# The W of two value heads in two PSUM banks, each with its own copy and its own count

## What is computed

```python
def step(S, xs):
    qt, kt, vt, gt, bt = xs
    S = S * jnp.exp(gt)[..., None, None]
    kS = jnp.einsum('bhk,bhkv->bhv', kt, S)
    S = S + bt[..., None, None] * kt[..., :, None] * (vt - kS)[..., None, :]
    o = jnp.einsum('bhk,bhkv->bhv', qt, S)
    return (S, o)
...
o = o * jax.lax.rsqrt(var + 1e-06) * norm_w * _silu(z)
return o.reshape(B, T, value_dim) @ W_out
```

## Time and profile before

| what | value |
|---|---|
| median of 3 runs | 2559.62 us (2553.06 to 2559.69) |
| the profiled execution, its own time | 2561.94 us |
| its span, first to last instruction | 2559.9 us |
| TensorE products busy | 2189.3 us (86%) |
| VectorE busy | 1676.1 us (65%) |
| ScalarE busy | 961.1 us (38%) |
| GpSimd busy | 701.5 us (27%) |
| chain that ended last | PE 44%, DVE 12%, ACT 3%, issue 3% |

### The profile page before, as it was taken

One profiled execution on the slowest core, in us unless ns is written; L12 is line 12 of the kernel. 1 busy time (PEld: TensorE's weight loads), 2 busy tenths in 40 slices (PEclk: granted clock), 3 DMA queues, 4 the chain that ended last, 5 costly groups with the idle time before them and its releaser, 6 DMA issues.

```text
span 2559.9 us, 41273 instructions
## 1 busy us (share of the span) xinstructions
PE 2189.3 (86%) x13086; PEld 1568.3 (61%) x13134; DVE 1676.1 (65%) x2777; ACT 961.1 (38%) x2492; POOL 701.5 (27%) x598
## 2 busy tenths in 40 slices
PE   3089989968884687799999999999999999999996
PEld 2044445433334343587787778778778778778776
DVE  7267777740014555678777777777877777777775
ACT  0000000017761001454454454455455445445444
POOL 8000000000001002342552452353354255245243
PEclk8589999989995799899999999999999999999998
DMA  2510000000000011000000000000000000000001
GB/s 63 57 37 18 18 31 23 20 7 0 0 0 20 27 31 54 21 13 29 25 18 23 25 33 12 29 25 12 29 25 12 29 25 12 29 25 24 17 25 33
DMA packets 24766, 61.01 MB, mean 24 GB/s; under 512 B 3315, under 2 KB 9731, under 8 KB 22563
## 3 DMA queue, kind: packets, MB, share of 16 engines
q1 hardware_dynamic: 24742, 60.72, 8.2%
HBM read 56.31 MB, written 4.40 MB: 24 GB/s over the span
## 4 chain that ended last, share of the span: by engine, by line
PE 44%; DVE 12%; ACT 3%; issue 3%; POOL 0%; DMA 0%; DVEq 0%; ACTq 0%; POOLq 0%
PE ps L1103 5%; PE ps L1231 4%; PE ps L1223 4%; PE ps L1141 4%; PE ps L1151 3%; DVE P L1634 3%; DVE P_term L1631 3%; DVE conv L1555 2%; PE ps L1288 2%; PE ps L1166 2%; PE ps L1277 2%; PE ps L1237 2%; PE ps L1177 2%; PE ps L1290 2%; PE ps L1264 2%
## 5 line engine op out<-in xcount | busy, mean ns | idle before, releaser
L1555 DVE SCALAR_TENSOR_TENSOR conv<-raw,tap_st,conv 128x1024 f32<-128x1024 f32 x204 | 300.0, 1470 | 3.8
L517 DVE TENSOR_REDUCE m_part<-ps 128x512 f32 (+3 forms) x384 | 208.3, 555 | 95.5 <-PE ps L444 58.0
L1103 PE MATMUL ps<-xnT,w_conv_st 128*128 128x512 f32 x544 | 250.3, 599 | 4.4 <-DMA w_conv_st<-in_w_conv 4.4
L456 PE MATMUL ps<-xnT,w_gate_up 128*128 128x512 f32 x384 | 203.9, 617 | 51.9 <-DMA w_gate_up<-in_gu 51.9
L1535 POOL TENSOR_TENSOR o<-o,silu_z 128x256 f32<-128x256 f32 x128 | 138.5, 1082 | 255.3 <-DVE silu_z L1575 141.7
L765 POOL MEMSET l_w3f<- 128x768 f32 x1 | 0.7, 738 | 718.6 <-POOLq L579 718.6
L496 ACT ACTIVATE tanh_g<-ps 128x512 f32<-128x512 f32 x48 | 28.7, 597 | 414.7 <-PE ps L456 414.7
L1308 ACT COPY raw<-ps 128x512 f32<-128x512 f32 x136 | 80.7, 593 | 271.2 <-PE ps L1103 271.2
L1429 POOL TENSOR_TENSOR gmask_Q<-upto,g 128x2048 f32<-128x2048 f32 x17 | 61.4, 3612 | 433.7 <-PE ps L1244 433.6
L670 ACT ACTIVATE probs<-ps 128x1024 f32<-128x1024 f32 (+7 forms) x256 | 145.9, 660 | 55.6 <-PE ps L628 35.2
L1515 POOL TENSOR_TENSOR kq_decayed<-conv,decay_rows 128x1024 f32<-128x1024 f32 x64 | 158.3, 2502 | 0.0
(11 more groups left out here) (306 smaller groups left out, 4944.4 us busy)
## 6 DMA issues: line engine op xcount, KB each, us to landing
decay_rows<-scratch_egc SPq DMA_DIRECT2D x17, 1024.0 KB, 4.7
w_conv_st<-in_w_conv SPq DMA_DIRECT2D x17, 512.0 KB, 3.3
w_gate_up<-in_gu SPq DMA_DIRECT2D x8, 768.0 KB, 4.3
w_out_st<-in_w_out SPq DMA_DIRECT2D x17, 256.0 KB, 2.6
w_z_st<-in_w_z SPq DMA_DIRECT2D x16, 256.0 KB, 2.6
q_stack<-scratch_q SPq DMA_DIRECT2D x6, 512.0 KB
w_down<-in_down SPq DMA_DIRECT2D x8, 384.0 KB, 3.0
l_w_gate_up<-in_gu SPq DMA_DIRECT2D x11, 256.0 KB, 2.6
```

What stands on the lines that cost most here:

```text
L456: mm = pe.matmul(ps[:, gb + which, :], wgu[:, k, which, tile * P:(tile + 1) * P], m.xnT[:, k, cols], start=k == 0, stop=k == KT - 1)
L517: dve.tensor_reduce(m.mpart[:, qt, bass.ds(i * REP + hh, 1), half:half + 1], ps[:, 6 + n_bank % 2, 0:cols], AX.X, ALU.max).then_inc(s_max, 1)
L1103: mm = pe.matmul(ps[:, 6 + n % 2, :], wc[:, k, (n // 2) * P:(n // 2 + 1) * P], m.xnT[:, k, (n % 2) * HALF:(n % 2 + 1) * HALF], start=k == ...
L1555: op = dve.scalar_tensor_tensor(out=cv[:, t, :], in0=raw[:, t, at:at + T], scalar=tap[:, t, at:at + 1], in1=cv[:, t, :], op0=ALU.mult, op1 ...
```

## The change

Head 0's W stays in bank 1, head 1's W goes to bank 0, each in columns 0 to 127. Each W product counts `s_w`, ScalarE copies each head's W by its own instruction as soon as its count is there and counts `s_wa` for each, and TensorE waits for head e's copy just before head e's state update (in chunk 7, just before head e's part of the outputs).

```diff
-        SU_BANK = (2, 0)
+        W_BANK, SU_BANK = (1, 0), (2, 0)
...
                     for e in range(2):
-                        mm = pe.matmul(ps[:, 1, e * P:(e + 1) * P], e_p[:, e, c, :], vnat[:, e, c, :], start=True, stop=True)
-                    mm.then_inc(s_w, 1)
+                        pe.matmul(ps[:, W_BANK[e], 0:P], e_p[:, e, c, :], vnat[:, e, c, :], start=True, stop=True).then_inc(s_w, 1)
...
                     if c == 0:
                         pe.wait_ge(s_ke, i * 2 + 2)
-                    pe.wait_ge(s_wa, i * NC + c + 1)
                     if c < NC - 1:
                         for e in range(2):
+                            pe.wait_ge(s_wa, i * 2 * NC + 2 * c + e + 1)
                             pe.matmul(ps[:, SU_BANK[e], 0:P], ke[:, e, c, :], wsb[:, e, :], start=True, stop=True).then_inc(s_su, 1)
                     for e in range(2):
+                        if c == NC - 1:
+                            pe.wait_ge(s_wa, i * 2 * NC + 2 * c + e + 1)
                         mm = pe.matmul(ps[:, bank, e * P:(e + 1) * P], ua[:, e, c, 0, :], wsb[:, e, :], start=c == 0, stop=c == 0 or e == 1)
                     mm.then_inc(s_aw, 1)
...
                 for c in range(NC):
-                    act.wait_ge(s_w, i * NC + c + 1)
-                    nc.scalar.copy(wsb[:].rearrange("p e n -> p (e n)"), ps[:, 1, 0:2 * P]).then_inc(s_wa, 1)
+                    for e in range(2):
+                        act.wait_ge(s_w, i * 2 * NC + 2 * c + e + 1)
+                        nc.scalar.copy(wsb[:, e, :], ps[:, W_BANK[e], 0:P]).then_inc(s_wa, 1)
```

## The result

The changed kernel takes 2571.76 us, the median of 8 runs (2564.45 to 2575.13), against 2560.13 for the kernel before in the same sessions (8 runs, 2553.06 to 2562.49). The ratio is 1.0042, 95% interval [1.0028, 1.0057]: slower by some 11 us, where 19 us less was forecast, and above the forecast range of 2535 to 2552. The profiled execution has a span of 2563.9 us, only 4.0 more than the one before. The part ahead of the first recurrence was shorter in it: the first W of the first head comes at 1101.1 us, before at 1107.3. From there to the end it is 1462.8 us against 1452.6.

The account below looks back on a forecast made before the run. The prediction took TensorE's waits for ScalarE's copy of W, 31.0 us in total, as what could be cut. (3 × 0.31 + 0.28) × 16 = 19.4 us gave 2540.2 us, range 2535 to 2552.

Parts of the forecast that it names:

- A 128-column copy and its overlap: ScalarE's half-size copies of W: 0.27 us each, the pair 0.43 us overlapped or 0.54 us not, against 0.37 before.
- Light chunks: Chunks 1, 2, 4 and 6, where two z passes leave W's copy exposed: 0.31 us gain each, range 0.20 to 0.34.
- The extra load time after a wait: TensorE loading update 1's weights without a product beside it: could make a light chunk's gain 0.10 us smaller.
- Heavy chunks: Chunks 0, 3 and 5, where four z passes hide W's copy: no gain and no loss.
- The convolution tap in chunk 2: VectorE's 1.63 us tap ahead of the state update: its 0.36 us idle room just fits the 0.32 us gain.
- Chunks 6 and 7 together: The last two chunks of a head, with ScalarE's tanh ahead of the last copy: 0.28 us gain, range 0.19 to 0.35.
- The recurrence in sum: Three light chunks at 0.31 us plus 0.28 us for chunks 6 and 7: 1.21 us gain per head.
- this too is handed on: End of a head's recurrence: the 0.28 us gain of chunks 6 and 7 passes into TensorE's first products of the next head.
- no clock effect is there to be won or lost: From 1107 to 2530 us TensorE is busy 1361.56 of 1423.00 us at full clock, so no clock term was counted.
- Rival 1: Gain cut at chunk 2's convolution tap and the head's end: 9.9 us remain, 2550 us; chance 0.13.
- Rival 2: ScalarE sees head 0's W no earlier than head 1's: at most 2.4 us gain, 2557 us; chance 0.09.
- Rival 3: TensorE's added wait brings a 0.24 us gap at seven updates and the last output: 11.4 us longer, 2571; chance 0.08.

Follow-up runs that it names:

- e7: e5 with VectorE's gate_outputs moved from chunk 6 to chunk 7; 2538.75 us, ratio 0.9925 to the kernel before.
- e8: e5 with one TensorE wait for both copies ahead of the first state update; 2548.42 us, ratio 0.9962 to the kernel before.
- e5: The changed kernel plus an idle 256-column memset on GpSimd ahead of its row of four products; 2539.86 us, ratio 0.9928 to the kernel before.
- e2: The kernel before, without the split, with GpSimd's third product held until VectorE's mask is made; 2561.06 us, ratio 1.0002.
- e6b: The kernel before, without the split, with one idle power instruction on GpSimd ahead of its row of products; 2587.95 us, ratio 1.0121.
- e9: The kernel before, without the split, with an idle 256-column memset on GpSimd ahead of its row of products; 2564.43 us, ratio 1.0021.
- e3: The kernel before, without the split, with a 256-column memset on VectorE ahead of its mask of U; 2560.77 us, ratio 1.0007.
- e1: The changed kernel with GpSimd's third product held until VectorE's mask is made; 2549.50 us, ratio 0.9956 to the kernel before.
- e4: e1 with one TensorE wait for both copies ahead of the first state update; 2549.73 us, ratio 0.9963 to the kernel before.

## Why the prediction was wrong

- *A 128-column copy and its overlap*: 0.27 us forecast, 0.266 measured; the pair 0.43 to 0.54, measured 0.49. Right.
- *Light chunks*: 0.31 us forecast, 0.35 measured in chunks 1, 2 and 4 (W to W 3.31 us instead of 3.66), just above my upper end of 0.34. The extra load time after a wait, my lower end, didn't show. *Heavy chunks* stayed at 3.64 to 3.87. The convolution tap in chunk 2 cost nothing, as argued.
- *Chunks 6 and 7 together*: 0.28 us forecast. Chunk 6 gave nothing, for a reason that I hadn't seen (gate_outputs behind GpSimd's o_rsqrt, e7); chunk 7 gave 0.33, of which TensorE hands on 0.12, by which the last copy of W ends earlier.
- *The recurrence in sum*: 1.21 us per head forecast, 1.17 measured. That it is so close is in part luck: three light chunks gave 0.12 more than forecast, chunks 6 and 7 gave 0.16 less.
- *The step that failed* is the one from the recurrence to the whole head: "TensorE goes from there into the next head's first products, which are on the chain, so this too is handed on", and with it the sum of 19.4 us, in which nothing else of the head changes. TensorE did hand on 1.17 of the 1.21 us. But I took the rest of the head as rigid. "Nothing moves in the queues of SyncE and GpSimd" was true of their order and false of their times: GpSimd's row came 0.22 us nearer to VectorE's mask, whose lead was 0.21 us, and the mask grew by 2.09 us. I had read no row of that place, though its long VectorE instructions (a sum of 256 columns that takes 2.46 us) stand in the trace of before.
- *A second term, put at nothing*, is the clock: "no clock effect is there to be won or lost". Full clock in the trace of before showed none to be won. After, TensorE's idle time ahead of line 1199 grew to 3.0 us, and 12 stretches ran at half clock. With the missed turn alone a head would take 92.9 us, as its three heads at full clock do, and 16 such heads would leave the time 2 us below that of before (an estimate); what the changed kernel takes beyond that came with the half clock.
- *Rival 1* named the right kind of cause, a gain cut on its way, with another mechanism and with no way to end above the time before. *Rival 2* fell: the first copy starts 0.28 us earlier behind W's weights. *Rival 3* gave 2571 us and was right in the number alone: the wait that it blames is worth a gain (e8 against e5), and seven updates per head show no such gap.
- With the port conflict put back as it was (e5), the same split measures 2539.86 us where 2540.2 was forecast.

## What to carry to other kernels

A gain in one engine's chain shifts it against the others for the rest of the loop, and in a loop without slack in its pattern each head repeats the same meeting, so a lead of 0.2 us can be worth 29 us in the sum (e5 against the changed kernel). Before summing such a gain, look behind the changed lines for instructions that take far longer than their size asks (here 2.46 us for 256 columns): they are places where two engines take turns, and the distance from the one's start to the other's is the margin. When a change loses time though its own place got faster, compare segment by segment, keep the repetitions at full clock apart from those with a stretch at half clock, and try an idle instruction on the engine that came too near.

## What the runs showed of the hardware

- A VectorE instruction that reads two SBUF tensors beside a GpSimd product of 2.35 us waits for that product's end: the mask takes 0.68 us alone, and 0.79, 1.04, 2.37 or 2.88 us depending on where in a product it falls. In the kernels before, changed, e2, e5, e6b, e7, e8 and e9 it ends 0.55 us behind the end of the product that ran at its start; e3, with a memset ahead of the mask, is the one exception. The product that comes next then waits in turn (2.80 us). The copy that makes P, with one SBUF input, is held too (1.84 us before, 0.28 in the changed kernel, where GpSimd's row is over by then). P_term, with a PSUM operand, isn't held (0.41 us in e1). The Trainium skill says it on the page "Advanced Engine Details and Errata", section "GPSIMD Details": GpSimd shares a read and a write interface with VectorE and conflicts with VectorE instructions in a 2-port mode or with two SBUF inputs. The rows of the mask, of the sum and of the subtraction agree. Whether the copy of P, with one input, runs in such a mode no row shows. That the turn lasts a whole GpSimd instruction is read from the rows above.
- TensorE ran on at 2.4 GHz after idling 1.8 us per head, and had stretches at 1.2 GHz in most heads after 3.0 us (12 of 15, changed). With 2.5 to 2.6 us it happened in some heads and not in others (e1 8, e2 3, e4 4, e6b 12). A stretch cost from nothing (some heads of e6b, 94.6 us with and without) to 2.2 us per head (changed, 95.1 against 92.9). So two kernels that differ by 8 us in their chains (e1 and e4) measured the same.
- TensorE's first weights of the next head come 0.50 to 0.53 us behind the end of the last copy of W in all eleven traces, with a gap of 0.16 us behind the weight loads between them (changed) or without one (before). What TensorE's sequencer does in those 0.5 us, no run here tried.
